# Turning keys, queries and values by way of DRAM and VectorE's 32x32 transposes, instead of by TensorE

## What is computed

```python
mixed = hidden_states @ W_qkv                       # q, k: 8 heads; v: 16 heads; width 128
mixed = causal_conv_silu(mixed)                     # 4 taps along the tokens
beta  = sigmoid(hidden_states @ W_b)
g     = -exp(A_log) * softplus(hidden_states @ W_a + dt_bias)
q, k  = l2norm(q) * DK ** -0.5, l2norm(k)           # each key head serves 2 value heads
def step(S, inp):                                   # for each of 2048 tokens, for each head
    S = S * exp(gt)
    v_adj = (vt - kt @ S) * bt
    S = S + outer(kt, v_adj)
    return S, qt @ S
o = rmsnorm(o) * norm_weight * silu(z)              # z = hidden_states @ W_z
s = o @ W_out
g = silu(sum_k rw_k * (gelu(x @ w1_k + b1_k) @ w2_k + b2_k))     # 2 experts
```

## Time and profile before

| | |
|---|---|
| median of three runs | 2064.51 us |
| profiled execution | 2060.95 us |
| its span, first to last instruction | 2059.2 us |
| TensorE busy | 1997.2 us (97%) |
| VectorE busy | 1337.3 us (65%) |
| ScalarE, GpSimd busy | 911.0 us (44%), 836.8 us (41%) |
| DMA packets | 388022, 184.25 MB |
| steps 3 to 30 | from 162.7 to 1110.9 us, 28 steps |

### The profile page before, as it was taken

How to read it: one execution, slowest core, us unless ns; L and a number is a source line. 1 busy time by engine, 2 the same in 40 slices (tenths; PEclk the granted TensorE clock), 3 DMA queues, 4 the chain that set the end, 5 groups by cost and what they waited for, 6 DMA issues and landing times.

```text
span 2059.2 us, 39550 instructions
## 1 busy us (share of the span) xinstructions
PE 1997.2 (97%) x13730; PEld 1705.4 (83%) x13730; DVE 1337.3 (65%) x3097; ACT 911.0 (44%) x2525; POOL 836.8 (41%) x2123
## 2 busy tenths in 40 slices
PE   5789999999999999999999999999999999999999
PEld 3578888888888888888888888888888888887887
DVE  6768887778787777887786445555555444447442
ACT  4465555555556565655554532222333233224221
POOL 2456576666666665757665411000111110111111
PEclk8899999999999999999999999999999999999999
DMA  4234444454336444444444223433334534303441
GB/s 131 47 74 81 102 87 96 82 94 83 93 84 106 82 98 92 86 92 84 97 80 85 84 82 72 92 78 76 83 80 84 123 82 103 72 21 123 154 149 66
DMA packets 388022, 184.25 MB, mean 89 GB/s; under 512 B 249456, under 2 KB 369136, under 8 KB 385776
## 3 DMA queue, kind: packets, MB, share of 16 engines
q1 hardware_dynamic: 354640, 177.73, 37.9%
q10 hardware_dynamic: 33184, 4.01, 1.3%
HBM read 135.26 MB, written 46.40 MB: 88 GB/s over the span
## 4 chain that ended last, share of the span: by engine, by line
PE 75%; issue 10%; DVE 6%; DMA 3%; POOL 3%; ACT 3%; SPq 1%; POOLq 0%; ACTq 0%; DVEq 0%
PE bank L333 18%; PE bank L335 18%; PE bank L334 18%; PE bank L565 3%; PE bank L574 2%; PE bank L548 2%; DMA VT<-v_dram 2%; PE bank L468 2%; PE bank L556 2%; PE bank L584 2%; PE bank L527 2%; PE bank L533 2%; POOL y_out L1825 1%; PE bank L502 1%; DVE cvx_k L1340 1%
## 5 line engine op out<-in xcount | busy, mean ns | idle before, releaser
L1771 POOL TENSOR_TENSOR prod<-A_in,V 128x60 f32<-128x60 f32 (+24 forms) x992 | 304.0, 306 | 270.6 <-DMA A_in<-a_dram 200.2
L1773 POOL TENSOR_TENSOR V<-V,prod 128x60 f32<-128x60 f32 (+24 forms) x992 | 311.6, 314 | 77.7
L1098 ACT ACTIVATE hid<-bank,bias 128x512 f32<-128x512 f32 x128 | 88.4, 691 | 455.0 <-PE bank L335 453.2
L1815 POOL TENSOR_TENSOR ffn_w_lo<-ffn_raw,ffn_w_hi 128x1024 fp32r<-128x1024 f32 x32 | 78.0, 2439 | 468.6 <-ACT ffn_w_hi L1088 464.7
L1563 DVE TENSOR_TENSOR h_lo<-hid,h_hi 128x512 fp32r<-128x512 f32 x128 | 91.1, 712 | 266.0 <-ACT h_hi L1105 266.0
L1577 DVE SCALAR_TENSOR_TENSOR gate_acc<-bank,rw,gate_acc 128x512 f32<-128x512 f32 x240 | 177.4, 749 | 58.8 <-PE bank L335 58.8
L333 PE MATMUL bank<-ffn_w_hi,h_hi 128*128 128x512 f32 x512 | 199.3, 389 | 1.3 <-DVE h_lo L1563 1.0
L333 PE MATMUL bank<-xn_hi,ffn_w_hi 128*128 128x512 f32 x512 | 200.3, 391 | 0.0
L335 PE MATMUL bank<-xn_hi,ffn_w_lo 128*128 128x512 f32 x512 | 199.3, 389 | 0.0
L334 PE MATMUL bank<-xn_lo,ffn_w_hi 128*128 128x512 f32 x512 | 199.2, 389 | 0.0
L334 PE MATMUL bank<-ffn_w_lo,h_hi 128*128 128x512 f32 x512 | 199.2, 389 | 0.0
(11 more groups left out here) (222 smaller groups left out, 5151.2 us busy)
## 6 DMA issues: line engine op xcount, KB each, us to landing
E<-eg_dram SPq DMA_DIRECT2D x64, 256.0 KB, 7.6
A_in<-a_dram SPq DMA_DIRECT2D x32, 512.0 KB, 4.0
decb<-dec_dram SPq DMA_DIRECT2D x128, 128.0 KB, 4.2
og_dram<-og SPq DMA_DIRECT2D x64, 256.0 KB, 2.2
ffn_raw<-w SPq DMA_DIRECT2D x32, 512.0 KB, 4.0
og_x<-og_dram SPq DMA_DIRECT2D x256, 64.0 KB, 2.6
ogT_dram<-og_y SPq DMA_DIRECT2D x64, 256.0 KB, 2.4
og_in<-ogT_dram SPq DMA_DIRECT2D x16, 1024.0 KB, 5.3
```

Of the source, the lines that this page charges most:

```text
L1098: act.activation(hid[:, i % 2, :], bank[i % 4][:, :], ACT.Gelu_apprx_tanh, bias=bias1[:, k, f * NF + ft:f * NF + ft + 1]).then_inc(S_["gel ...
L1771: pool.tensor_tensor(prod[:, 0:m, 0:n], column, V[:, vb, 0:m, j:j + 1].to_broadcast([P, m, n]), MUL).then_inc(S_["product"], 1)
L1773: pool.tensor_tensor(V[:, vb, 0:m, j + 1:B32], V[:, vb, 0:m, j + 1:B32], prod[:, 0:m, 0:n], ADD).then_inc(S_["solve_step"], 1)
L1815: pool.tensor_tensor(fw[m, "lo", n % 2][:, :], raw[:, i % 2, :], fw[m, "hi", n % 2][:, :].bitcast(f32), SUB).then_inc(S_["ffn_lo"], 1)
```

## The change

TensorE's three turning functions go. In their place:

- ScalarE stores the values `vS` (128x1024) to DRAM (`store_v`, second quarter, behind the activation of v1), and SyncE loads them with four DMAs in an order in which only 32x32 blocks are left to turn (`load_v`, behind the two later `decb`); rows of 32 elements, 128 bytes, 1024 to a DMA.
- SyncE stores keys with queries of block st as one 128x1024 tile (`load_kq`, fourth quarter, behind the store of `og`), waits for this store, and loads it in the same way. It is used a step later.
- VectorE turns the 32x32 blocks: `turn_kq` in the second quarter, behind the convolution of k and ahead of the third `chain_R`; `turn_v` in the fourth quarter, behind `gated` and `scan` and ahead of the fourth `chain_S`. Each is two instructions of 128x512.
- ScalarE's `squares_q` goes from the first quarter to the third (for the block before), and both halves of `put_v` from the second and third to the fourth, ahead of the last `mean_squares` and of `put_y64`. All three and `put_k` work in SBUF now.
- ScalarE's writes of `vS` and of `kqT` wait for the DMAs of the block that lay there. `og` has one buffer instead of two, `v_tok` too; V64 and Y64 are one tile, so `put_y64` and `diagonal` write VY64.
- In the prologue the same functions stand for blocks 0 and 1.

```diff
@@ buffers @@
-        V64 = alloc(p2b, "V64", [NCH, 2 * B32])
+        VY64 = alloc(p2b, "VY64", [NCH, 2 * B32])
         Y32 = alloc(p2b, "Y32", [NCH, B32])
-        Y64 = alloc(p2b, "Y64", [NCH, 2 * B32])
-        v_tok = alloc(p2b, "v_tok", [2, CPS, REP * HD])
+        kq_x = alloc(p2b, "kq_x", [NQD * 2 * CPS, B32])
+        v_x = alloc(p2b, "v_x", [NQD * REP * CPS, B32])
         z_gate = alloc(p2b, "z_gate", [2, CPS, REP * HD])
-        k_rem = alloc(p2b, "k_rem", [2, CPS, REP, HD])
-        og = alloc(p2b, "og", [2, 2, REP, HD])
+        qd = alloc(p2b, "qd", [2, REP, P])
+        k_rem = [alloc(p2b, "k_rem0", [CPS, REP, HD])]
+        R = alloc(p2b, "R", [REP, HD])
         U = alloc(p2b, "U", [2, REP, HD])
+        k_rem.append(alloc(p2b, "k_rem1", [CPS, REP, HD]))
+        og = alloc(p2b, "og", [2, REP, HD])
         squares = alloc(p2b, "squares", [REP, HD])
+        S = alloc(p2b, "S", [REP, HD])
+        v_tok = alloc(p2b, "v_tok", [REP, CPS, HD])
@@ TensorE @@
                 if is_block(st - 1):
-                    pe.wait_ge(S_["v_tok"], 2 * st)
+                    pe.wait_ge(S_["z_gate"], CPS * (st - 1) + 3)
...
-            def turn_q(st):
-                b = st
...
-            def turn_k(st):
-                b = st - 1
...
-            def turn_v(st, half):
-                b = st - 1
...
-                if now:
-                    turn_q(st)
...
-                if turned:
-                    turn_v(st, 0)
...
-                if turned:
-                    turn_v(st, 1)
-                    turn_k(st)
@@ ScalarE @@
-            def squares_q(st):
-                b = st
+            def squares_q(b):
                 act.wait_ge(S_["q_turned"], b + 1)
                 for c in range(CPS):
-                    turned = TQ_BANK[:, c * P:(c + 1) * P]
+                    turned = kq_x[:, :, :].rearrange("p (b c a) j -> p a c b j", b=NQD, a=2)[:, 0, c, :, :]
                     i = act.activation(turned, turned, ACT.Square, accum_out=q_sq[:, b % 4, c:c + 1])
                 i.then_inc(S_["q_sq"], 1)
...
                 b = st - 1
                 act.wait_ge(S_["k_turned"], b + 1)
                 act.wait_ge(S_["c_rem"], b + 1)
-                if b >= 2:
-                    act.wait_ge(S_["state_add"], CPS * (b - 1))
                 for c in range(CPS):
-                    for h in range(REP):
-                        i = act.mul(k_rem[:, b % 2, c, h, :], TK_BANK[:, c * P:(c + 1) * P], c_rem[:, b % 4, c, h:h + 1])
+                    for h in (1, 0):
+                        i = act.mul(k_rem[b % 2][:, c, h, :], k_rem[b % 2][:, c, 0, :], c_rem[:, b % 4, c, h:h + 1])
                 i.then_inc(S_["k_rem"], 1)
             def put_v(st, half):
                 b = st - 1
-                act.wait_ge(S_["v_turned"], 2 * b + half + 1)
+                act.wait_ge(S_["v_turned"], b + 1)
                 if b >= 2:
                     act.wait_ge(S_["factor"], 2 * (b - 2) + 1)
                 else:
                     act.wait_ge(S_["k_len"], b + 1)
-                if b >= 2:
-                    act.wait_ge(S_["R"], CPS * (b - 1))
                 for i in range(2):
                     c = 2 * half + i
-                    r = act.mul(v_tok[:, b % 2, c, :], TV_BANK[half][:, i * REP * HD:(i + 1) * REP * HD], roots[:, b % 4, c:c + 1])
+                    r = act.mul(v_tok[:, :, c, :], v_tok[:, :, c, :], roots[:, b % 4, c:c + 1])
                 r.then_inc(S_["v_tok"], 1)
+
+            def store_v(b):
+                act.wait_ge(S_["act_v0"], b + 1)
+                act.wait_ge(S_["act_v1"], b + 1)
+                if b:
+                    act.wait_ge(S_["v_turned"], b)
+                else:
+                    act.wait_ge(S_["xT"], 14)
+                act.dma_start(vs_dram.rearrange("i b t -> b i t"), vS[:, :, :].rearrange("p h t -> p (h t)")).then_inc(S_["v_x"], 16)
...
                     put_z64(st - 2)
-                if now:
-                    squares_q(st)
                 if turned:
                     silu(st - 1, "v0")
...
                 if turned:
                     silu(st - 1, "v1")
+                    store_v(st - 1)
                 if chain:
                     chain_U(st - 2, 1)
...
                 if chain:
                     mean_squares(st - 2, 1)
-                if turned:
-                    put_v(st, 0)
                 if ahead:
...
                     mean_squares(st - 2, 2)
                 if turned:
-                    put_v(st, 1)
+                    squares_q(st - 1)
                     put_k(st)
                 if st == NU:
...
                         split_weights(group * len(PARTS) + n)
                 if turned:
                     put_z32(st - 1)
+                    put_v(st, 0)
+                    put_v(st, 1)
                 if chain:
                     mean_squares(st - 2, 3)
@@ VectorE @@
+            def turn_kq(b):
+                dve.wait_ge(S_["kq_x"], X_SET * (b + 1))
+                if b >= 2:
+                    dve.wait_ge(S_["state_add"], CPS * (b - 1))
+                elif b:
+                    dve.wait_ge(S_["rows_out"], 32 * NSB)
+                kq = kq_x[:, :, :].rearrange("p (b c a) j -> p a c b j", b=NQD, a=2)
+                dve.transpose(k_rem[b % 2][:, :, 0, :].rearrange("p c (b j) -> p c b j", b=NQD), kq[:, 0, :, :, :]).then_inc(S_["k_turned"], 1)
+                dve.wait_ge(S_["k_turned"], b + 1)
+                dve.transpose(kq[:, 0, :, :, :], kq[:, 1, :, :, :]).then_inc(S_["q_turned"], 1)
+
+            def turn_v(b):
+                dve.wait_ge(S_["v_x"], X_SET * (b + 1))
+                if b:
+                    dve.wait_ge(S_["R"], CPS * b)
+                for h in range(REP):
+                    src = v_x[:, :, :].rearrange("p (b m) j -> p m b j", b=NQD)[:, h * CPS:(h + 1) * CPS, :, :]
+                    r = dve.transpose(v_tok[:, h, :, :].rearrange("p c (b j) -> p c b j", b=NQD), src)
+                r.then_inc(S_["v_turned"], 1)
...
-                if p >= 2:
-                    dve.wait_ge(S_[f"og_out{p % 2}"], 16 * (p // 2))
+                if p:
+                    dve.wait_ge(S_[f"og_out{(p - 1) % 2}"], 16 * ((p - 1) // 2 + 1))
...
-                if now:
-                    query_norms(st)
                 if ahead:
                     convolve(st + 1, "k")
+                if turned:
+                    turn_kq(st - 1)
...
+                if turned:
+                    turn_v(st - 1)
                 if now and st % NSB == 2 and st // NSB + 1 < KEY_HEADS:
                     for n in range(2):
                         split_weights((st // NSB + 1) * len(PARTS) + n)
                 if chain:
                     chain_S(st - 2, 3)
+                if turned:
+                    query_norms(st - 1)
                 if now:
@@ SyncE @@
+            def load_kq(b):
+                sp.wait_ge(S_["act_k"], b + 1)
+                sp.wait_ge(S_["act_q"], b + 1)
+                if b:
+                    sp.wait_ge(S_["q_sq"], b)
+                else:
+                    sp.wait_ge(S_["xT"], 12)
+                sp.dma_start(kq_dram.rearrange("i b t -> b i t"), kqT[:, b % KQ_LIFE, :, :, :].rearrange("p c a t -> p (c a t)")).then_inc(S_["kq_x"], 16)
+                sp.wait_ge(S_["kq_x"], X_SET * b + 16)
+                for q in range(NQD):
+                    r = slice(q * B32, (q + 1) * B32)
+                    src = kq_dram.rearrange("i b (m t) -> i (b m) t", t=P)[:, :, r]
+                    sp.dma_start(kq_x[r, :, :], src).then_inc(S_["kq_x"], 16)
+
+            def load_v(b):
+                sp.wait_ge(S_["v_x"], X_SET * b + 16)
+                for q in range(NQD):
+                    r = slice(q * B32, (q + 1) * B32)
+                    src = vs_dram.rearrange("i b (m t) -> i (b m) t", t=P)[:, :, r]
+                    sp.dma_start(v_x[r, :, :], src).then_inc(S_["v_x"], 16)
...
                 next_decay(2)
                 next_decay(3)
+                if turned:
+                    load_v(st - 1)
                 if now and st % NSB == 1 and group + 1 < KEY_HEADS:
...
                 if chain:
                     store(2 * (st - 2))
+                if now:
+                    load_kq(st)
                 if st == NU - 1:
```

More of the change, by code:

```diff
@@ L75 @@
 ffn_bias ffn_bias1 ffn_raw0 ffn_raw1 wo_raw og_raw0 og_raw1 og_turned0 og_turned1 og_in0 og_in1 og_in2 x_res0 x_res1 out0 out1
-rows_out eg0 eg1 dec0 dec1 begin0 begin1 a_out a_in v_out vt_in
+rows_out eg0 eg1 dec0 dec1 begin0 begin1 a_out a_in v_out vt_in v_x kq_x
 xT smallT ab_turned sums score_parts scores_sum rows_turned
-proj_k proj_q proj_v0 proj_v1 z_proj k_turned q_turned v_turned pair_kq keys queries solved state_add out_add lev_y32 lev_z32 lev_y64 lev_z64
+proj_k proj_q proj_v0 proj_v1 z_proj pair_kq keys queries solved state_add out_add lev_y32 lev_z32 lev_y64 lev_z64
 sw_hi xn_hi ab_T ab_in exp_steps exp_sum rows
```

(38 more changed lines are left out.)

90 lines of the change are left out of this document (36 added, 54 removed).

## The result

The changed kernel takes 2313.82 us (median of 4, 2304.55 to 2320.20) against 2064.87: ratio 1.120, with a 95% interval of 1.116 to 1.124. Slower was right; 2120 and the range up to 2210 were far too low. The profiled execution has a span of 2318.4 us.

The account below looks back on a forecast made before the run. TensorE's own work was taken to bound each 33.86 us step; -0.44 + 0.5 + 0.2 + 0.8 + 0.7 = +1.76 us a step, 58 with the prologue, gave 2120 us, with an 8-in-10 range of 2042 to 2210.

Parts of the forecast that it names:

- The store's bytes: Values' store, 512 KB in the full DMA stretch: 1.8 us of all queues, making VT, E and decb late; +0.8 a step.
- second rival: Values' store runs on 4 queues, delaying VT, E, decb, v_x: +2.7 to 5.4 us a step, 2200 to 2290; chance 0.22.
- the 0.8 for VT: VectorE waits longer for VT, landing up to 1.8 us later behind the values' store: +0.8 us a step, between 0 and 4.
- the signs: Profile tests: no VectorE wait for v_x meant the first rival's time; E and VT over 4 us later, the second rival's.
- first rival: The cover holds: v_x lands before 669 and VT is little later; 2035 to 2055, say 2048; chance 0.19.
- SyncE's wait for the store: Fourth quarter, keys with queries: store lands in 4.0 us, next decb still in time; cost 0, up to 2 a step.
- turn_kq ahead of R, +0.5: Two VectorE transposes, 1.4 us, ahead of the third R with 0.89 slack: TensorE waits +0.5 us a step, bounds 0 to 1.4.
- The store's issue ahead of U, +0.2: ScalarE's DMA issue, taken as 0.7 us, between vS and U: +0.2 us a step, between 0 and 0.8.
- Late values, +0.7: Fourth quarter: v_x lands after the scan ends, delaying S, keys and put_y64; +0.7 us a step, bounds 0 and 2.2.
- TensorE's transposes: 16 a step, 1.76 us, leave TensorE; some only filled waits, so -0.44 us a step, turn_q's gain counted with late values.
- The prologue, +3: Prologue: SyncE waits for two stores, 4.0 us each, partly beside other work; +3 us in all, 0 to 8.
- the forecast's case: The summed terms hold: +1.76 us a step, 2120 us, own range 2085 to 2155; chance 0.53.

Follow-up runs that it names:

- dead_store: Only keys and queries by DRAM (2081.77 us), plus the values' store as one DMA ahead of U that nothing reads: 2214.39 us.
- dead_store16: As dead_store, but the values' store that nothing reads is issued as four DMAs of 32 partitions: 2134.67 us.
- kq_split: The changed kernel with SyncE's wait for the store of keys with queries, and its loads, moved to the next step: 2245.25 us.
- quarters_kq: The changed kernel with only the store of keys with queries issued as four DMAs of 32 partitions: 2161.98 us.
- gap: As only_kq, with turn_kq moved behind the third R and variance, ahead of the scans: 2072.05 us, ratio 1.0033.
- only_kq: Half the change: keys and queries by DRAM, stored in four DMAs; values turned by TensorE, put_v at its old places: 2079.01 us, ratio 1.0085.
- quarters: The changed kernel with both stores (values, keys with queries) issued as four DMAs of 32 partitions each: 2157.65 us, ratio 1.0465.
- late_store: As quarters, with the values' four store DMAs moved from ahead of the second chain_U to behind the second mean_squares: 2170.21 us, ratio 1.0474.
- halves: The changed kernel with both stores issued as two DMAs of 64 partitions each, destination 2 x 32 x 1024: 2511.04 us.

## Why the prediction was wrong, step by step

- **The store's bytes: the step that failed.** The prediction says "the bytes take 1.8 us of all queues". They take 4 queues; the store of keys and queries landed after 10.9 us, and the values' hold up A_in (9.8 us and not 4.0) and E (10.4 and not 7.6). I had this as the second rival with a chance of 0.22 and priced it at 2200 to 2290. Against it I put that no row showed such a DMA and that the queues as a whole were 0.86 busy; neither speaks against it. dead_store shows it alone: +133 us.
- **Who is late first.** I followed VT and v_x. E has less slack: VectorE waited for it already in 16 steps before (1.16 us in step 17), and its scans stand ahead of S. With the store on all queues (dead_store16) neither is waited for longer than without it: the 0.8 for VT should have been 0, too. So two of the signs misled. VectorE hardly waits for v_x, which was to mean the first rival's time, and its waits for VT don't rise; E and VT land 6.1 and 5.5 us later in the step, which was the second rival's sign, and that one held.
- **SyncE's wait for the store, "Cost 0".** That was reckoned for a wait of 4.0 us, and it was 10.9. It put A_in behind the values' store: some 70 us by kq_split, 152 by quarters_kq, where the store's 4 queues are gone too.
- **The clock.** No term for it. It costs TensorE 60 us in the 28 steps, and follows the idle time that the other terms make.
- **turn_kq ahead of R, +0.5.** Right, in size and mechanism: TensorE waited 13.9 us for R in 28 steps, 0.5 each; 0.54 by gap against only_kq.
- **The store's issue ahead of U, +0.2.** Small and right in kind: 10.5 us in 28 steps, 0.4. Split in four, it is the largest wait left (52.4 us in 28 steps in quarters).
- **Late values, +0.7.** Not reached in the change, since the steps were longer by more for E. late_store shows it: 58.7 us of waits for v_x.
- **TensorE's transposes.** Their 1.76 us a step stand in the account above (49.3 us) as read from the kernel before; no run measures them apart. That much of this is no gain, as the forecast had it, shows in gap, where 8 transposes less a step (24.6 us in 28 steps) shorten the steps by 9.5.
- **The prologue, +3.** It was +18.7, and 20.7 more came behind the 28 steps. No run takes the 18.7 apart.
- Without the 4 queues, the forecast's case is quarters: 2157.65, above 2120 and just outside that case's own range. There the largest wait is that for U behind ScalarE's four issues, which the forecast's kernel doesn't have; but moving them away (late_store) brought no gain, so how near that forecast would have come without them stays open. Slower would have been right without the 4 queues too, but 156 of the 249 us came by the second rival's mechanism and not by the forecast's.

## What to carry to other kernels

Read the outermost dimension of every DMA's destination (the side that these runs vary) before its bytes are priced: with 4 there the store kept 20.8% of the queues busy, and what was queued behind it, A_in, E and the fourth VT, landed late. Price a DMA in a full stretch by the transfer with the least slack behind it, and look at which of them it comes to stand ahead of: about 3 us of delay on the issuing engine turned the order of two transfers, and with it the kernel went from about 100 us above the one before (quarters_kq) to 250. And where TensorE starts to wait for microseconds, add the time that it then runs at half clock.

## What was not expected of the hardware

- A store with 2, 4 or 32 outermost kept 12.2%, 20.8% and 96.9% of the 16 queues busy; two of the first kind at once (halves) didn't spread over others.
- After 5.0 us without a product (step 17 of the change), TensorE ran for 4.9 us at a granted clock of 0.50; 4 us of useless products ahead of the wait (filler) brought the mean of the 28 steps from 0.92 to 0.99.
